# Attention probabilities turned in 32 × 32 blocks on VectorE and placed by sixteen DMAs, with the value product one unit later

## The chip, the cores and the metric

The kernel runs on one core of a Trainium2 chip. The metric is the device time of one execution, in microseconds (us). An engine's name is followed here by what it does in this kernel: TensorE (PE) multiplies and transposes, VectorE (DVE) and ScalarE (ACT) move results out of PSUM and do the softmax, GpSimd (POOL) does small sums, splits and gathers, and SyncE (SP) issues transfers.

## The reference, cut to what matters

Three small layers with adapters produce x (8 sequences of 128 rows, 512 columns); an attention with a paged cache follows. The part around the change is, for each of 8 sequences and each of 8 key heads (4 query heads share one key head):

```python
k_all = concatenate([kc, k], axis=1)          # 512 cached keys and 128 new ones
v_all = concatenate([vc, v], axis=1)
scores = einsum('bqhd,bkhd->bhqk', q, k_all) * SCALE
scores = where(valid, scores, -1e30)
probs = softmax(scores, axis=-1)
attn = einsum('bhqk,bkhd->bqhd', probs, v_all)
out = attn.reshape(bsz, seqlen, -1) @ Wo.T    # summed over the heads
```

with q and k projected from x, normalized by their root mean square and rotated. The result is added to x.

## The kernel before

The attention runs over 64 units, a unit being one sequence and one key head with its 4 query heads. Each engine has its own instruction stream, a loop over the units whose body is that engine's `step`; the order in each is written out by hand, and semaphores tie them together. A float32 product that needs full precision is made of three float32r products (`three`): each operand is split in a rounded high part and the rest (`..._hi`, `..._lo`). ScalarE writes the high part of a PSUM tile and VectorE the rest.

In step n TensorE computes the scores of two heads (`score_pair`, 12 products), eight of the twelve products of the next unit's queries, the scores of the other two heads, the other four query products, the output product of unit n−1 (`put_out`, 12 products), and the transposes of unit n's probabilities (`turn_probs`, five chunks of keys by four heads, 20 in all) alternating with the value products (`values`, 15 of 512 columns). Between these it projects the next unit's new key and value (`project_new_key`, 12 products of 256 columns) and transposes its rotated queries and key (`turn_rotated`) and the cached keys of the unit after (`turn_cached`). The turned probabilities pass through two PSUM banks, `ps_ring`; ScalarE copies each (`chunk_high`, tile pt_hi) and VectorE subtracts (`chunk_low`, tile pt_lo). The softmax takes, for each head, a masked minimum on VectorE (`lowest`, L1112), the exponential on ScalarE (`exps`, L622), the reciprocal of the sum on VectorE (`inverse`), and the scaling on ScalarE (`normalize`, L627). The keys' path is key square on ScalarE (L585), `variances` and `rotate_key` on VectorE (L1061 to L1073), a power on GpSimd (`norm_factors`), `scale_key` on ScalarE (L603), the transpose, then `rotated_high` on ScalarE and `rotated_low` on VectorE. SP loads the next unit's x_s (L335) when its key product is done, and a chunk of later weights (L338). Line 1028 is VectorE's subtraction of any tile (`rest`), L582 ScalarE's copy of any tile.

Of the kernel before, what the change touches and what calls it, by code (L numbers as in the profile page):

```python
# [13 lines left out]
P = 128  # L14
# [17 lines left out]
AHEAD = B + 1  # L32
THETA = 10000.0
# [13 lines left out]
def build(nc, x, x_t, ids0, ids1, ids2, table, lens, w0_t, bias0, lora_a, lora_b, w1_t, w2_b, w2_a,  # L47
          w_qkvo, q_norm, k_norm, k_rows, v_rows, inv_freq, row_in_table, ident_in, out):
    ctx = ExitStack()
    with ctx:  # L50
# [142 lines left out]
        with ExitStack() as p2:  # L193

            rot_a = sb("rot_a", [P, GROUP + 1, D], scope=p2)
# [13 lines left out]
            v_hi = sb("v_hi", [P, CH, D], F32R, scope=p2)  # L209
            v_lo = sb("v_lo", [P, CH, D], F32R, scope=p2)  # L210
            prob = sb("prob", [P, GROUP, KEYS], scope=p2)
            pt_hi = sb("pt_hi", [P, CH, GROUP * P], F32R, scope=p2)
            pt_lo = sb("pt_lo", [P, CH, GROUP * P], F32R, scope=p2)
            ot_hi = sb("ot_hi", [P, GROUP * P], F32R, scope=p2)
            ot_lo = sb("ot_lo", [P, GROUP * P], F32R, scope=p2)
            mask = sb("mask", [P, KEYS], scope=p2)
# [21 lines left out]
            v_hi_out, v_split, vn_hi_out, vn_lo_out = (psem(s) for s in ("v_round", "v_split", "vn_hi_out", "vn_lo_out"))  # L238
            scores, low_done, exp_done, inv_done, prob_done = (psem(s) for s in ("scores", "low_done", "exp_done", "inv_done", "prob_done"))
            p_turned, pt_hi_out, pt_lo_out = psem("p_turned"), psem("pt_hi_out"), psem("pt_lo_out")  # L240
# [9 lines left out]
            def keys_of(kt, u, lo, hi):  # L250

                return kt[:, bass.ds((u & 1) * KEYS + lo, hi - lo)]

# [3 lines left out]
            with nc.Block() as block:  # L257
                @block.sync
                def _(sp):
# [71 lines left out]
                    def step(n, weights, last, finished):  # L331
                        if not last:
                            sp.wait_ge(kv_proj, n + 1)
                            sp.nop(nofuse=True)
                            sp.dma_start(x_s[:, :, :].bitcast(F32), xt_dram[bass.ds((n + 1) & 7, 1), :, :, :].rearrange("a p s c -> p (a s) c")).then_inc(x_s_in, 16)  # L335
                        if weights:
                            sp.wait_ge(w_split, n + AHEAD)
                            sp.dma_start(w_raw[:, 0, :], w_qkvo[bass.ds(n + AHEAD, 1), :, :].rearrange("a p c -> p (a c)")).then_inc(w_raw_in, 16)  # L338
                        if finished:
                            sp.wait_ge(y_added, n)  # L340
                            sp.nop(nofuse=True)
                            sp.dma_start(out[bass.ds((n - 1) & 7, 1), :, :].rearrange("a p c -> p (a c)"),
                                         y[:, bass.ds((n - 1) & 7, 1), :].rearrange("p a c -> p (a c)")).then_inc(out_in, 16)

                    sp.wait_ge(xt_stored, 32)
                    step(0, True, False, False)
                    sp.wait_ge(xt_stored, 16 * B)
                    with sp.Fori(1, UNITS - AHEAD) as n:
                        step(n, True, False, False)
                    with sp.Fori(UNITS - AHEAD, UNITS - B + 1) as n:  # L350
                        step(n, False, False, False)
                    with sp.Fori(UNITS - B + 1, UNITS - 1) as n:
                        step(n, False, False, True)
                    step(UNITS - 1, False, True, True)
                    step(UNITS, False, True, True)
# [3 lines left out]
                def _(pool):  # L359
# [108 lines left out]
                    def step(n, weights, keys, last):  # L468

                        vl = v_lo[:, 0:CCH, :].rearrange("p c d -> p (c d)")  # L470
                        vh = v_hi[:, 0:CCH, :].rearrange("p c d -> p (c d)")
# [3 lines left out]
                        pool.wait_ge(v_hi_out, n + 1)  # L475
                        nc.gpsimd.tensor_tensor(vl, v_raw[:, :], vh.bitcast(F32), ALU.subtract).then_inc(v_split, 1)  # L476
                        if not last:
                            next_values(n + 1)
                        if keys:
                            next_keys(n + 2)  # L480
# [7 lines left out]
                    with pool.Fori(0, UNITS - AHEAD) as n:  # L488
# [4 lines left out]
                    step(UNITS - 1, False, False, True)  # L493

                @block.scalar
                def _(act):
# [108 lines left out]
                    def cached_high(u, first=False):  # L605
# [3 lines left out]
                        copy(keys_of(kt_hi, u, 0, CACHE), ps_ring[:, 0, :]).then_inc(kc_hi_out, 1)  # L609
# [6 lines left out]
                    def out_high(u):  # L616
                        act.wait_ge(pv_done, u + 1)
                        copy(ot_hi[:, :], ps_o[:, :]).then_inc(ot_hi_out, 1)
# [10 lines left out]
                    def chunk_high(n, c, bank):  # L629
                        act.wait_ge(p_turned, CH * n + c + 1)  # L630
                        copy(pt_hi[:, c, :], ps_ring[:, bank, :]).then_inc(pt_hi_out, 1)

                    def step(n, keys, last, first=False):
                        if first:
                            cached_high(1, first=True)
                        else:
                            out_high(n - 1)
# [627 lines left out]
```

## Time and profile before

| | |
|---|---|
| median of 3 runs | 1242.81 us (1242.17 to 1243.01) |
| the profiled execution | 1239.95 us |
| its span, first to last instruction | 1238.1 us |
| busy: TensorE, VectorE, ScalarE, GpSimd | 98%, 74%, 69%, 44% |
| mean granted clock of TensorE | 0.993 of full speed |
| data moved by DMA | 109.5 MB, 88 GB/s on the mean |

The span is what the profile shows of one execution; the time of that execution is a little longer, and the runs that give the median were other executions. Busy means that an instruction of the engine was in progress; matmuls overlap, so a busy TensorE says that it was never without one. Each row of the timeline gives the start, the length, the engine and the line, and the output and inputs.

### The profile page before, as it was taken

The page shows a single profiled execution, that of the slowest core. Times are in us where ns is not written, and L with a number is a line of the kernel's source. Part 1 is how long each engine was busy: PE and PEld are TensorE (multiplying, and loading weights), DVE is VectorE, ACT ScalarE, POOL GpSimd, SP SyncE. Part 2 cuts the span into 40 slices and gives each one's busy share as a digit, 9 for nine tenths or more (in the row PEclk, how much of TensorE's full clock was granted, in tenths as well). Part 3 has the DMA queues.
Part 4 walks back from the last instruction along what each step waited for, and adds up shares of the span by engine and source line. Part 5 has one row for each costly group of instructions (what it writes and reads, how often), then busy time and mean ns, then how long its engine had stood idle before and what let it go on. Part 6 is the DMA issues. An engine that isn't in the chain of part 4 may idle for free.

```text
span 1238.1 us, 28992 instructions
## 1 busy us (share of the span) xinstructions
PE 1212.0 (98%) x7072; PEld 1038.2 (84%) x7072; DVE 918.8 (74%) x2295; ACT 853.2 (69%) x2170; POOL 545.5 (44%) x570
## 2 busy tenths in 40 slices
PE   7998999999999999999999999999999999999997
PEld 4565888888888888888888888888888888888885
DVE  2336778777778777787787877877778777777774
ACT  2233777777777777777777777777777777767774
POOL 7761444445444444444444444444544445333430
PEclk9998999999999999999999999999999999999999
DMA  6673222222222222222122222222222222112210
GB/s 193 232 255 107 78 67 78 89 89 67 75 80 89 89 62 80 80 89 89 61 74 87 89 86 65 72 89 89 78 67 77 89 89 69 63 59 85 85 52 25
DMA packets 37607, 109.50 MB, mean 88 GB/s; under 512 B 7512, under 2 KB 7640, under 8 KB 36570
## 3 DMA queue, kind: packets, MB, share of 16 engines
q1 hardware_dynamic: 25288, 68.44, 16.1%
q0 software_dynamic: 11152, 36.72, 10.4%
q10 hardware_dynamic: 1154, 4.19, 0.9%
q8 instruction: 6, 0.10, 0.0%
q14 instruction: 7, 0.06, 0.0%
HBM read 103.03 MB, written 6.29 MB: 88 GB/s over the span
## 4 chain that ended last, share of the span: by engine, by line
PE 96%; DVE 1%; ACT 1%; DMA 1%; issue 1%; POOL 0%; SPq 0%; DVEq 0%; ACTq 0%; POOLq 0%
PE ps_q L794 14%; PE ps_ring L858 12%; PE ps_o L694 11%; PE ps_o L696 11%; PE ps_o L695 11%; PE ps_kv L794 7%; PE ps_s L696 6%; PE ps_s L694 6%; PE ps_s L695 6%; PE ps_l L726 2%; PE ps_ring L820 2%; PE ps_q L828 2%; PE ps_t L688 1%; PE ps_l L742 1%; PE ps_h L712 1%
## 5 line engine op out<-in xcount | busy, mean ns | idle before, releaser
L622 ACT ACTIVATE prob<-prob,low 128x640 f32<-128x640 f32 x256 | 210.8, 824 | 129.0 <-DVE low L1112 128.9
L1028 DVE TENSOR_TENSOR pt_lo<-ps_ring,pt_hi 128x512 fp32r<-128x512 f32 x320 | 209.1, 686 | 87.8 <-ACT pt_hi L582 87.5
L1112 DVE CUSTOM_DVE_ANT_0 prob<-ps_s,mask,q_gain 128x640 f32<-128x640 f32 x256 | 216.3, 882 | 36.8 <-PE ps_s L696 35.0
L103 POOL TENSOR_TENSOR w_lo<-w_raw,w_hi 128x640 f32 (+1 forms) x64 | 100.2, 1565 | 263.6 <-DVE w_hi L97 262.3
L582 ACT ACTIVATE pt_hi<-ps_ring 128x512 fp32r<-128x512 f32 x320 | 181.5, 593 | 33.1 <-PE ps_ring L858 33.0
L627 ACT ACTIVATE prob<-prob,inv 128x640 f32<-128x640 f32 x256 | 196.9, 818 | 0.0
L858 PE MATMUL ps_ring<-ident,prob 128*128 128x128 f32 x1280 | 186.3, 276 | 5.1 <-DVE pt_lo L1028 2.7
L858 PEld LDWEIGHTS ps_ring<-ident,prob 128*128 128x128 f32 x1280 | 149.0, 141 | 40.3 <-DVE pt_lo L1028 9.9
L794 PE MATMUL ps_q<-w_hi,x_s 128*128 (+1 forms) x512 | 171.8, 396 | 0.0
L694 PE MATMUL ps_s<-kt_hi,qt_hi 128*128 (+1 forms) x512 | 159.4, 311 | 1.5 <-DVE low L1112 1.5
L696 PE MATMUL ps_s<-kt_hi,qt_lo 128*128 (+1 forms) x512 | 159.5, 311 | 0.0
L695 PE MATMUL ps_s<-kt_lo,qt_hi 128*128 (+1 forms) x512 | 159.1, 311 | 0.0
L476 POOL TENSOR_TENSOR v_lo<-v_raw,v_hi 128x512 fp32r<-128x512 f32 x64 | 83.4, 1302 | 154.6 <-DVE v_hi L1085 154.6
L694 PE MATMUL ps_o<-pt_hi,v_hi 128*128 128x512 f32 x320 | 147.6, 461 | 0.0
L696 PE MATMUL ps_o<-pt_hi,v_lo 128*128 128x512 f32 x320 | 126.9, 397 | 0.0
L695 PE MATMUL ps_o<-pt_lo,v_hi 128*128 128x512 f32 x320 | 125.6, 392 | 0.0
L466 POOL TENSOR_TENSOR rstd<-var,neg_half 128x5 f32<-128x5 f32 x64 | 77.4, 1209 | 85.9 <-DVE var L1061 85.8
L794 PEld LDWEIGHTS ps_q<-w_hi,x_s 128*128 128x128 f32 x512 | 95.6, 188 | 15.0
L794 PE MATMUL ps_kv<-w_hi,x_s 128*128 (+1 forms) x512 | 106.8, 293 | 0.0
L694 PEld LDWEIGHTS ps_s<-kt_hi,qt_hi 128*128 128x128 f32 x512 | 97.0, 189 | 7.5 <-DVE low L1112 1.8
L694 PE MATMUL ps_o<-w_hi,ot_hi 128*128 (+1 forms) x256 | 101.0, 394 | 1.4 <-DVE ot_lo L1028 1.4
L695 PEld LDWEIGHTS ps_s<-kt_lo,qt_hi 128*128 128x128 f32 x512 | 96.9, 189 | 5.7
(141 smaller groups left out, 2587.8 us busy)
## 6 DMA issues: line engine op xcount, KB each, us to landing
x_s<-xt_split SPq DMA_DIRECT2D x64, 512.0 KB, 3.3
w_raw<-w_qkvo_dram SPq DMA_DIRECT2D x55, 320.0 KB, 3.5
w<-w_t_dram SPq DMA_DIRECT2D x8, 1024.0 KB, 6.8
xt_split<-x3t ACTq DMA_DIRECT2D x8, 512.0 KB, 4.3
w_raw<-w_qkvo_dram POOLq DMA_DIRECT2D x9, 320.0 KB, 4.9
xbt<-x_t_dram SPq DMA_DIRECT2D x8, 256.0 KB, 2.9
xb<-x_dram SPq DMA_DIRECT2D x8, 256.0 KB, 3.7
out_dram<-y SPq DMA_DIRECT2D x8, 256.0 KB, 2.2
```

What stands on the lines that cost most here:

```text
L103: return nc.gpsimd.tensor_tensor(lo, raw, hi.bitcast(F32), ALU.subtract)
L476: nc.gpsimd.tensor_tensor(vl, v_raw[:, :], vh.bitcast(F32), ALU.subtract).then_inc(v_split, 1)
L582: return nc.scalar.activation(dst, src, ACT.Copy)
L622: nc.scalar.activation(prob[:, h, :], prob[:, h, :], ACT.Exp, bias=low[:, h:h + 1], scale=-1.0, accum_out=total[:, h:h + 1]).then_inc(exp_ ...
L627: nc.scalar.activation(prob[:, h, :], prob[:, h, :], ACT.Copy, scale=inv[:, h:h + 1]).then_inc(prob_done, 1)
L694: nc.tensor.matmul(dst, lh, rh, start=first, stop=False)
L695: nc.tensor.matmul(dst, lh, rl, start=False, stop=False)
L696: return nc.tensor.matmul(dst, ll, rh, start=False, stop=final)
L794: mm = nc.tensor.matmul(dst, x_s[:, int(i % 3 == 2), k * P:(k + 1) * P], w_rest if i % 3 == 1 else w, start=i == 0, stop=i == 3 * KT - 1)
L858: mm = nc.tensor.transpose(ps_ring[:, bank, h * P:(h + 1) * P], prob[:, h, c * P:(c + 1) * P], ident[:, :])
L1028: return nc.vector.tensor_tensor(dst, src, high.bitcast(F32), ALU.subtract)
L1112: nc.vector.tensor_tensor_reduce(out=prob[:, h, :], in0=ps_s[:, score_slot(h):score_slot(h) + KEYS], in1=mask[:, :], scale=q_gain[:, h:h + ...
```

## The change

The probabilities are no longer transposed by TensorE. VectorE turns each head's 128 × 640 probabilities in 32 × 32 blocks (`turn_blocks`), which leaves every block in the group of 32 partitions where it was, and sixteen DMAs on SP's queue (`place_blocks`: 4 source groups by 4 destination groups, each 32 partitions of 2560 bytes) carry the blocks to where a transpose would have put them, in one of two halves of `prob_t` (alternating by unit). The source `blocks` is a single buffer, so the first turn of the next unit waits for all sixteen.

The value product takes `prob_t` and the values as plain float32, with one product in place of three, in two halves of two heads (256 columns) and five chunks each: ten instructions. It belongs to the unit before and stands last in TensorE's step; the output product belongs to two units before. Its second half uses the PSUM bank `ps_o1`, in which the cached keys of the next unit are turned before, so it waits until VectorE has taken those (`kc_lo_out`). The splits of the values (v_hi, v_lo, on VectorE and GpSimd) and of the turned probabilities are gone; ScalarE copies the new value to `v_next` and GpSimd from there to `v_new`. The gather of a unit's cached values moves from the step before to the step in which they are used. The query products are no longer cut in eight and four but all stand between the score pairs; the key product and the turning of the cached keys follow the second score pair. On ScalarE the squares move ahead of the exponentials of heads 2 and 3. On SP the x_s load is asked for before the sixteen transfers of the same step.

The diff, cut to its core. Blank lines and, outside TensorE's step, most removed lines are left out; the functions that they stand in are printed above. Indentation is shortened.

```diff
-ps_ring = pb("ps_ring", [P, 2, 512], p2)
+ps_x = pb("ps_x", [P, 512], p2)
+ps_o0 = pb("ps_o0", [P, 512], p2)
 ps_q = pb("ps_q", [P, 512], p2)
 ps_kv = pb("ps_kv", [P, 512], p2)
-ps_o = pb("ps_o", [P, 512], p2)
+ps_o1 = pb("ps_o1", [P, 512], p2)
+ps_o = (ps_o0, ps_o1)
...
+PAIR = 2 * P
+RUN = CH * GROUP * BLOCK
+def place_block(issuer, n, a, j):
+    issuer.dma_start(prob_t[j * BLOCK:(j + 1) * BLOCK, bass.ds((n & 1) * NB * RUN + a * RUN, RUN)],
+             blocks[a * BLOCK:(a + 1) * BLOCK, j, :, :, :].rearrange("p c h q -> p (c h q)")).then_inc(pt_in[j], 16)
+def turned_probs(u, c, pair):
+    half = prob_t[:, bass.ds((u & 1) * NB * RUN, NB * RUN)]
+    return half.rearrange("p (a c h q) -> p h a c q", a=NB, c=CH, h=GROUP)[:, 2 * pair:2 * pair + 2, :, c, :]
+def next_value(u):
+    return v_next[:, bass.ds((u & 1) * D, D)]
...
+def place_blocks(n, first=False):
+    sp.wait_ge(blocks_turned, GROUP * (n + 1))
+    sp.nop(nofuse=True)
+    if not first:
+        sp.wait_ge(pv_done, 2 * (n - 1))
+        sp.nop(nofuse=True)
+    for a in range(NB):
+        for j in range(NB):
+            place_block(sp, n, a, j)
...
+def step(n, inputs, weights, finished, first=False):
+    if inputs:
+        next_input(n + 2)
     if weights:
+        next_weights(n + 1)
+    place_blocks(n, first)
     if finished:
+        store_out(n - 2)
...
-    pool.wait_ge(v_split, u)
+    pool.wait_ge(pv_done, 2 * u)
...
+def move_new_value(u, values):
+    pool.wait_ge(vn_out, u + 1)
+    if values:
+        pool.wait_ge(pv_done, 2 * u)
+    pool.nop(nofuse=True)
+    nc.gpsimd.tensor_copy(v_new[:, :], next_value(u)).then_inc(vn_moved, 1)
+def step(n, weights, keys, last, first=False, second=False):
+    if not first:
+        move_new_value(n - 1, not second)
+        if not second:
+            next_values(n - 1)
     if weights:
         pool.wait_ge(w_rounded, n + AHEAD + 1)
         weight_low(n + AHEAD, w_raw[:, 0, :]).then_inc(w_split, 1)
     if not last:
         sum_queries(n + 1)
         norm_factors(n + 1)
+    if keys:
+        next_keys(n + 2)
...
+def step(n, last, head=True, out=True, first=False):
+    if head:
+        out_high(n - 2, 1, first=first)
     exps(n, 0)
     exps(n, 1)
     normalize(n, 0)
     normalize(n, 1)
+    if not last:
+        query_squares(n + 1, range(GROUP))
+        key_squares(n + 1)
+        new_value(n + 1, first=not out)
     exps(n, 2)
     exps(n, 3)
     normalize(n, 2)
+    if not last:
+        scale_key(n + 1)
+        cached_high(n + 1, ps_o1, first=not out)
     normalize(n, 3)
     if not last:
         rotated_high(n + 1)
+    if out:
+        out_high(n - 1, 0, first=not head)
...
+def values(u, cached, first=False):
+    pe.wait_ge(v_in, 16 * (u + 1))
+    pe.wait_ge(vn_moved, u + 1)
+    for j in range(NB):
+        pe.wait_ge(pt_in[j], 16 * NB * (u + 1))
+    if not first:
+        pe.wait_ge(ot_lo_out, 2 * u)
+    for pair in (0, 1):
+        if pair == 1:
+            pe.wait_ge(kc_lo_out, cached)
+        for c in range(CH):
+            v = v_raw[:, c * D:(c + 1) * D] if c < CCH else v_new[:, :]
+            mm = nc.tensor.matmul(ps_o[pair][:, 0:PAIR], v, turned_probs(u, c, pair),
+                                  start=c == 0, stop=c == CH - 1)
+        mm.then_inc(pv_done, 1)
...
+def step(n, last, out=True, pv=True, first=False):
     pe.wait_ge(qt_lo_out, n + 1)
     pe.wait_ge(kc_lo_out, n + 1)
     score_pair(n, 0)
     if not last:
         project_queries(n + 1)
     score_pair(n, 1)
     if not last:
-        project_queries_rest(n + 1)
-    if not first:
-        put_out(n - 1)
-    early, late = range(GROUP - 1), (GROUP - 1,)
-    pe.wait_ge(prob_done, GROUP * n + GROUP - 1)
-    turn_probs(n, 0, 1, early)
-    pe.wait_ge(kc_lo_out, n + 1 if last else n + 2)
-    turn_probs(n, 1, 0, early)
-    pe.wait_ge(prob_done, GROUP * n + GROUP)
-    turn_probs(n, 0, 1, late)
-    turn_probs(n, 1, 0, late)
-    if not last:
         project_new_key(n + 1)
-    pe.wait_ge(v_split, n + 1)
-    pe.wait_ge(vn_lo_out, n + 1)
-    if not first:
-        pe.wait_ge(y_added, n)
-    pe.wait_ge(pt_lo_out, CH * n + 1)
-    turn_probs(n, 2, 1)
-    values(n, 0)
-    pe.wait_ge(pt_lo_out, CH * n + 2)
-    turn_probs(n, 3, 0)
-    values(n, 1)
-    pe.wait_ge(pt_lo_out, CH * n + 3)
-    turn_probs(n, 4, 1)
+        turn_cached(n + 1, ps_o1, 2 * (n - 1) if out else None)
+    if out:
+        put_out(n - 2, first=first)
     if not last:
         turn_rotated(n + 1)
-    values(n, 2)
-    if keys:
-        pe.wait_ge(pt_lo_out, CH * n + 4)
-        turn_cached(n + 2)
-    values(n, 3)
-    values(n, 4)
+    if pv:
+        values(n - 1, n + 1 if last else n + 2, first=not out)
...
+def turn_blocks(n, h, first=False):
+    dve.wait_ge(prob_done, GROUP * n + h + 1)
+    if h == 0 and not first:
+        for j in range(NB):
+            dve.wait_ge(pt_in[j], 16 * NB * n)
+    nc.vector.transpose(blocks[:, :, :, h, :].rearrange("p j c q -> p c j q"),
+                        prob[:, h, :].rearrange("p (c j k) -> p c j k", c=CH, j=NB)).then_inc(blocks_turned, 1)
+def step(n, weights, last, head=True, out=True, first=False):
+    if head:
+        out_low(n - 2, 1)
+    dve.wait_ge(mask_set, n + 1)
+    dve.wait_ge(gain_done, n + 1)
+    if not first:
+        dve.wait_ge(blocks_turned, GROUP * n)
+    lowest(n, 0)
+    lowest(n, 1)
     if weights:
         weights_high(n)
     inverse(n, 0)
     inverse(n, 1)
+    if not last:
+        rotate_queries(n + 1)
+        rotate_queries_rest(n + 1)
     lowest(n, 2)
     lowest(n, 3)
+    turn_blocks(n, 0, first)
     if not last:
         variances(n + 1)
         rotate_key(n + 1)
+    turn_blocks(n, 1)
+    inverse(n, 2)
+    inverse(n, 3)
+    if head:
+        add_out(n - 2)
+    turn_blocks(n, 2)
     if not last:
         rotated_low(n + 1)
         gains(n + 1)
+    turn_blocks(n, 3)
+    if not last:
+        cached_low(n + 1, ps_o1)
+    if out:
+        out_low(n - 1, 0)
```

## Rows read from the trace of the kernel before

**Rows 1.** The page: busy us (share) of each engine; the chain that ended last.

```profile
PE 1212.0 (98%) x7072; PEld 1038.2 (84%) x7072; DVE 918.8 (74%) x2295; ACT 853.2 (69%) x2170; POOL 545.5 (44%) x570
...
PE 96%; DVE 1%; ACT 1%; DMA 1%; issue 1%; POOL 0%; SPq 0%; DVEq 0%; ACTq 0%; POOLq 0%
```

**Rows 2.** TensorE's timeline, one unit: start us, us, engine, line, operation.

```profile
606.76 0.28 PE L694 MATMUL ps_s<-kt_hi,qt_hi 128*128 x1
...
613.11 0.40 PE L694 MATMUL ps_o<-w_hi,ot_hi 128*128 x1
...
615.87 1.03 PE L858 MATMUL ps_ring<-ident,prob 128*128 128x128 f32 x8
616.66 0.36 PE L794 MATMUL ps_kv<-w_hi,x_s 128*128 x1
...
618.04 0.28 PE L794 MATMUL ps_kv<-w_hi,x_s 128*128 x1
```

**Rows 3.** VectorE's timeline, the same unit.

```profile
612.76 0.88 DVE L1112 CUSTOM_DVE_ANT_0 prob<-ps_s,mask,q_gain 128x640 f32<-128x640 f32 x1
...
618.76 0.17 DVE L1061 TENSOR_SCALAR var<-sq 128x5 f32<-128x5 f32 x1
...
619.69 0.68 DVE L1028 TENSOR_TENSOR pt_lo<-ps_ring,pt_hi 128x512 fp32r<-128x512 f32 x1
...
622.51 0.69 DVE L1028 TENSOR_TENSOR qt_lo<-ps_q,qt_hi 128x512 fp32r<-128x512 f32 x1
623.12 0.28 DVE L1028 TENSOR_TENSOR kt_lo<-ps_kv,kt_hi 128x128 f32 x1
623.32 0.16 DVE L1078 TENSOR_SCALAR q_gain<-rstd 128x4 f32<-128x4 f32 x1
623.39 0.48 DVE L1032 TENSOR_SCALAR mask<-pos,len_f 128x512 f32<-128x512 f32 x1
623.95 0.49 DVE L97 CAST w_hi<-w_raw 128x640 f32 x1
```

**Rows 4.** ScalarE's timeline, the same unit.

```profile
611.04 1.54 ACT L627 ACTIVATE prob<-prob,inv 128x640 f32<-128x640 f32 x2
...
618.36 0.28 ACT L585 ACTIVATE junk<-ps_kv 128x128 f32<-128x128 f32 x1
...
620.31 0.40 ACT L603 ACTIVATE rot<-key_sum,rstd 128x128 f32<-128x128 f32 x1 [0.80 <-POOL rstd L466]
620.62 1.15 ACT L582 ACTIVATE pt_hi<-ps_ring 128x512 fp32r<-128x512 f32 x2
621.72 0.60 ACT L582 ACTIVATE qt_hi<-ps_q 128x512 fp32r<-128x512 f32 x1
```

**Rows 5.** Timelines: the first score product of units 0 and 63; ScalarE's last normalizations.

```profile
119.49 0.56 PE L694 MATMUL ps_s<-kt_hi,qt_hi 128*128 128x256 f32 x1
...
1212.42 0.28 PE L694 MATMUL ps_s<-kt_hi,qt_hi 128*128 128x256 f32 x1
...
1220.08 1.53 ACT L627 ACTIVATE prob<-prob,inv 128x640 f32<-128x640 f32 x2
```

**Rows 6.** TensorE's timeline in the layers before the attention.

```profile
43.23 3.70 PE L726 MATMUL ps_l<-w,x1t 128*128 128x512 f32 x8
46.86 1.12 PE L742 MATMUL ps_l<-a,h 16*128 16x512 f32 x2
```

**Rows 7.** SP's timeline: four issues in a row at the start.

```profile
1.28 1.84 SPq L298 DMA_DIRECT2D y<-w_t_dram  x4
```

**Rows 8.** DMA issues: count, KB each, us from issue to landing.

```profile
x_s<-xt_split SPq DMA_DIRECT2D x64, 512.0 KB, 3.3
...
a<-lora_a_dram SPq DMA_DIRECT2D x8, 32.0 KB, 2.4
```

**Rows 9.** TensorE's timeline; then a stretch, PEclk its granted clock.

```profile
130.51 1.24 PE L858 MATMUL ps_ring<-ident,prob 128*128 128x128 f32 x8 [2.10 <-ACT prob L627]
...
130.00:135.00 5.00, 4.49 (x25) 4.41 (x26) 2.29 (x8) 3.56 (x14) 1.58 (x2) 0.66 0.21 60
```

More of the change, by code:

```diff
@@ L345, in _ @@
                     sp.wait_ge(xt_stored, 32)
-                    step(0, True, False, False)
+                    next_input(1)
+                    next_weights(0)
                     sp.wait_ge(xt_stored, 16 * B)
-                    with sp.Fori(1, UNITS - AHEAD) as n:
-                        step(n, True, False, False)
[L350 to L353, printed above, removed]
@@ L487, in _ @@
                     next_keys(1)
-                    with pool.Fori(0, UNITS - AHEAD) as n:
+                    step(0, True, True, False, first=True)
+                    step(1, True, True, False, second=True)
+                    with pool.Fori(2, UNITS - AHEAD) as n:
                         step(n, True, True, False)
@@ L627, in normalize @@
                         nc.scalar.activation(prob[:, h, :], prob[:, h, :], ACT.Copy, scale=inv[:, h:h + 1]).then_inc(prob_done, 1)
[L629 to L637, printed above, removed]
+                    def step(n, last, head=True, out=True, first=False):
+                        if head:
+                            out_high(n - 2, 1, first=first)
                         exps(n, 0)
                         exps(n, 1)
-                        act.wait_ge(kv_proj, n + 1)
-                        copy(v_hi[:, CCH, :], ps_kv[:, D:2 * D]).then_inc(vn_hi_out, 1)
                         normalize(n, 0)
                         normalize(n, 1)
+                        if not last:
+                            query_squares(n + 1, range(GROUP))
+                            key_squares(n + 1)
+                            new_value(n + 1, first=not out)
                         exps(n, 2)
@@ L854, in put_out @@
                         mm.then_inc(out_proj, 1)
-                    def turn_probs(n, c, bank, heads=range(GROUP)):
-                        for h in heads:
-                            mm = nc.tensor.transpose(ps_ring[:, bank, h * P:(h + 1) * P], prob[:, h, c * P:(c + 1) * P], ident[:, :])
-                        if h == GROUP - 1:
-                            mm.then_inc(p_turned, 1)
-                    def values(n, c):
-                        pe.wait_ge(pt_lo_out, CH * n + c + 1)
-                        mm = three(ps_o[:, :], (v_hi[:, c, :], v_lo[:, c, :]), (pt_hi[:, c, :], pt_lo[:, c, :]),
-                                   c == 0, c == CH - 1)
-                        if c == CH - 1:
-                            mm.then_inc(pv_done, 1)
@@ L870, in step @@
-                    def step(n, keys, last, first=False):
-                        if first:
-                            pe.wait_ge(kc_lo_out, 1)
-                            turn_cached(1)
+                    def step(n, last, out=True, pv=True, first=False):
                         pe.wait_ge(qt_lo_out, n + 1)
@@ L1188, in _ @@
                     set_mask(0)
-                    step(0, True, False, first=True)
-                    with dve.Fori(1, UNITS - AHEAD) as n:
+                    step(0, True, False, head=False, out=False, first=True)
+                    step(1, True, False, head=False)
+                    with dve.Fori(2, UNITS - AHEAD) as n:
                         step(n, True, False)
```

203 lines of the change are left out of this document (92 added, 111 removed).

## The prediction

> **What bounds the kernel now.** I read the page's busy shares and its chain of waits first [rows 1]: TensorE is busy 98% of the span and is 96% of the chain that ended last, while VectorE and ScalarE are busy 74% and 69%. Next came one unit on TensorE's timeline [rows 2]: its products follow one another without a gap. The reader is to see the stretches: from the first score product to the first output product (both score pairs and all twelve query products) 613.11 − 606.76 = 6.35 us; the twelve output products 2.76 us (0.23 us each); eight transposes of probabilities 0.79 us (0.10 each); the twelve key/value products from 616.66 to the end of the last, 618.04 + 0.28 = 618.32, 1.66 us. Then VectorE's and ScalarE's timelines of the same unit [rows 3, 4], for the length of each step and the time from the start of an instruction to the start of the one that waited for it. The first score product of unit 0 starts at 119.49 and that of unit 63 at 1212.42 [rows 5]: 17.35 us a unit over 63 steps. Because TensorE never waits, a unit costs the sum of its products. The question about the change is whether that stays so.
>
> **What the change takes from TensorE.** Per unit go 20 transposes at 0.10 to 0.11 us (2.1 us) and 15 float32r value products at 0.23 (3.45) [rows 2], 5.6 us in all. In come ten plain float32 products of 256 columns. The layers before the attention show this kind with 512 columns: four of them (eight records) start at 43.23 and the next group at 46.86, 0.91 us each [rows 6]. Half the columns is 0.45 us, ten are 4.5 us. TensorE's own work falls by 1.1 us, to 16.2 us a unit. That would be a time of 119.5 + 63 × 16.2 + 31.5 + 4.8, about 1176 us, if nothing else bound (the last terms are derived below).
>
> **What it does to the order.** TensorE now ends a step with the second half of the previous unit's value product. It shares its bank with the turned cached keys, so it waits for cached_low(n+1), which VectorE runs after the fourth turn_blocks(n). The next unit's scores are queued behind that half on TensorE. So everything from the scores of unit n to VectorE's last steps stands in one line. I add it up from the first score product of step n (time 0):
> - scores, queries (all twelve, now between the two score pairs), scores, then the key/value product: 6.35 + 1.66 + 0.04 for the hand-over = 8.05 [rows 2, 4].
> - ScalarE: the key square now stands ahead of exps 2 and 3, with the copy of the new value behind it: 0.28 + 0.29 = 8.62 [rows 4] (a 128-column copy takes about what the square takes).
> - VectorE: variances and rotate_key, 619.69 − 618.76 = 0.93 [rows 3], to 9.55; then turn_blocks 1. No row shows a block turn. It reads and writes 640 columns in SBUF. Bounds: the cast of 640 columns takes 0.49, the masked-minimum over 640 columns 0.88 [rows 3]. A two-operand step of 512 columns occupies the engine 0.61 (0.81 with the 128-column one of about 0.20 behind it), which scaled to 640 is 0.76. I take 0.76, since such a turn should pass one column after another. At 10.3 inverse 2 can start.
> - ScalarE: 0.17 later normalize 2 (0.73 of the pair's 1.54), scale_key 0.31, cached_high 0.50, normalize 3 0.73, rotated_high until VectorE can start 0.79 [rows 3, 4]: 13.5. The exponentials 2 and 3 (at 8.5 and 9.3, 0.83 each) fit beside turn_blocks 1. The output product, from about 8.3 to 11.1, and its add lie beside this too.
> - VectorE: rotated_low 0.81, gains 0.07, turn_blocks 3 0.76, cached_low 0.69 and an allowance of 0.15 until TensorE's product starts: 16.0 [rows 3].
> - TensorE: five products of 0.45, 2.25: 18.3.
>
> A unit thus costs 18.3 us, 2.1 more than TensorE's work and 0.95 more than now. With turns of 0.49 (two on the line, and less for what they hide) it would be 17.7, with 0.88 18.5; both are above 17.35. Most of the five evictions that leave ScalarE (pt_hi, about 0.55 each [rows 4]) and VectorE (0.6 each) buy nothing on this line: the four turns take their place on VectorE, and ScalarE waits about a microsecond for the key product. The vector copy v_hi, GpSimd's subtraction v_lo and the small v_lo go at no gain, since none ends a wait on the line; GpSimd's new copy and its gather of values at the start of the step have until 12 us, its pieces with the landing of 3.3 us being over by about 5.
>
> **The sixteen transfers.** Each moves 32 partitions × 2560 B = 82 KB, 1.31 MB a unit. They are issued on SP after turn_blocks 3; the first turn of the next unit waits for all of them, because it overwrites their source. Four issues in a row start 0.46 us apart [rows 7]; small transfers land in 2.4 us and the 512 KB one in 3.3 [rows 8]. So they take 16 × 0.45 + 0.1 + 2.5 = 9.8 us. Turn 3 ends at about 15.2. Turn 0 of the next unit is due when the fourth masked minimum ends, 18.3 + 7.8 = 26.1 (it starts at 612.76, 6.0 after the first score product [rows 2, 3], here one us later for the four query products moved ahead, and takes 0.8): 10.9 us of room, 1.1 to spare. Above that each microsecond goes into the unit whole. The loads of x_s (next_input) and weights are queued behind them on SP; the issues end 4 us into the next step, the key product that next_input also waits for at 8, so they lose nothing. Upper bound from rows: 2.4 to 3.3 us for 480 KB more is 0.15 us for 82 KB over 128 partitions; if 32 partitions are served four times slower, 0.6 us, 16 of them with landing are 12.2 us. I take the issue rate and keep 12.2 for the range. The Trainium skill (SBUF — State Buffer, Door 1: The DMA port swizzle) says that 32 partitions reach half of the 16 ports, measured at 189 GB/s. An estimate by it is 0.43 us for each transfer, as long as its issue, so that the x_s, weight and gather traffic on the same engines would decide; no run here shows such a transfer yet. That sentence speaks against the change.
>
> **Sum.** 119.5 to the first scores (unchanged) + 63 × 18.3 = 1152.9. From the last unit's first score product to the end is 1238.1 − 1212.4 = 25.7 now. Then: probabilities normalized as now at 1221.6 (+9.2 [rows 5]), last turn +0.8, transfers 9.8, ten products 4.5, eviction in two parts 0.9, output 2.9 + 0.3, add 0.7, store 2.4: 31.5. Span 1303.9. The profiled execution took 1239.95, 1.85 over its span, and the median of the runs lies 2.9 above it: 1308.7, so 1309 us. Unit 0 pays its cold start as now. The break-even is 17.25 us a unit.
>
> **Rivals.**
> - *The line is as added up*: 1309, with the bounds of the turns 1271 to 1322. Chance 0.58.
> - *The transfers bind.* For it: 1.1 us of room only, 1.3 MB of other traffic a unit by the tiles' sizes, the gather of values within these 10 us. Against: issue 0.45 each. At 12.2 the unit costs 12.2 + 7.4 = 19.6 (turn 0's 0.76 and from there the line above to the end of turn 3, 15.2 − 8.6), time 1394 with the later end; at 11.5, 1347. Served slower still by the other traffic, 1420. Chance 0.22.
> - *Block turns at half rate*, 1.5 us. Now three of them are on the line: 20.4 a unit, 1441. No row shows one. The Trainium skill (VectorE: DVE Perf Modes, The three transpose paths) gives 311 ns for 128 columns; an estimate by it for 640 is 1.56 us. Against, every VectorE row here passes about a column a nanosecond. Chance 0.07.
> - *Faster: plain float32 products of 256 columns pass at the float32r rate*, about 0.13 us (twelve key/value products of 256 columns in 1.66 [rows 2]). Pair 1 then costs 0.65 instead of 2.25, the unit 16.7, time 1208. It decides from 0.24 us a product down. Against: 0.91 at 512 columns [rows 6]. With whatever else makes the line at least 1.05 us shorter than I read it, chance 0.09; a further 0.01 for no change.
> - *The clock falls.* TensorE would idle 2.1 us a unit in two or three gaps. After 128.4 to 130.5, 2.1 us without work, the mean granted clock was 0.66, partly at the lower level of 1.2 GHz [rows 9]. One such stretch a unit makes about 3.4 us of products take twice as long, half of it on the line: 20.0 a unit, 1416. The gaps are split, so 0.03.
>
> Chances: slower 0.88, within 0.2% 0.03, faster 0.09 (0.2% is about what a measurement of this kernel can tell; a spread of the first case or of the fast one near the break-even gives the 0.03). The range 1268 to 1420 holds the first case with its bounds, the second and the clock's. It leaves out the fast case, no change and the slow turns, 0.17, and some edges of the rest. The likeliest case alone spans 1271 to 1322.
>
> **What would show it.** In the profile after: TensorE near 88% busy, with idle time before the second value half put down to VectorE's kt_lo, and a little before the rotated transposes; the chain passing through VectorE and ScalarE; ScalarE's key square waiting about 1 us for ps_kv; block turns near 0.76 to 0.85 us; plain products 0.45 us apart; SP issues 0.45 us apart; no VectorE wait on the transfers. If turn 0 waits for a transfer, the second case holds and my landing time is wrong. If TensorE stays gapless at 16.2 us a unit, I have read the order wrongly.

## The result and the profile after

The changed kernel takes 1412.07 us (median of 4 runs, 1410.91 to 1414.47), against 1242.49 for the kernel before, run in between. The ratio is 1.1374, with a 95% interval of 1.1348 to 1.14: 170 us slower. The recorded forecast was 1309, 67 us slower, in a range of 1268 to 1420.

The page of the changed kernel, busy shares and chain, to be laid beside [rows 1]:

```profile
PE 1219.1 (86%) x6112; PEld 1013.1 (72%) x6112; DVE 855.5 (61%) x2167; ACT 685.0 (49%) x1914; POOL 475.6 (34%) x570
SPq 39%; issue 19%; DVE 11%; PE 11%; DMA 9%; ACT 7%; DVEq 2%; ACTq 0%; POOL 0%; POOLq 0%
L1156 DVE STREAM_TRANSPOSE blocks<-prob 128x640 f32<-128x640 f32 x256 | 215.1, 841 | 109.2 <-DMA prob_t<-blocks 92.5
```

TensorE has lost its 96% of the chain; SP's queue, which before had 0% of it, holds 39%, and the block turns wait 92.5 us for transfers. SP's timeline shows two units:

```profile
676.20 10.49 SPq L264 DMA_DIRECT2D prob_t<-blocks  x16
...
695.91 10.50 SPq L264 DMA_DIRECT2D prob_t<-blocks  x16
...
715.62 10.49 SPq L264 DMA_DIRECT2D prob_t<-blocks  x16
```

The batches start 715.62 − 695.91 = 19.71 us apart, and 695.91 − 676.20 = 19.71 before that: that is a unit. Between 400 and 1000 us most units take just this and some up to 20.1. Sixteen issues take 10.5 us. VectorE's timeline between those batches, the four turns and the two subtractions about the last:

```profile
705.53 0.88 DVE L1137 CUSTOM_DVE_ANT_0 prob<-ps_s,mask,q_gain 128x640 f32<-128x640 f32 x1
...
707.99 0.84 DVE L1156 STREAM_TRANSPOSE blocks<-prob 128x640 f32<-128x640 f32 x1 [1.57 <-DMA prob_t<-blocks]
708.76 0.13 DVE L1092 TENSOR_SCALAR var<-sq 128x5 f32<-128x5 f32 x1
...
709.58 0.84 DVE L1156 STREAM_TRANSPOSE blocks<-prob 128x640 f32<-128x640 f32 x1
...
711.36 0.85 DVE L1156 STREAM_TRANSPOSE blocks<-prob 128x640 f32<-128x640 f32 x1 [0.25 <-ACT prob L692]
713.50 0.69 DVE L1058 TENSOR_TENSOR qt_lo<-ps_q,qt_hi 128x512 fp32r<-128x512 f32 x1 [1.29 <-ACT kt_hi L640]
...
714.38 0.84 DVE L1156 STREAM_TRANSPOSE blocks<-prob 128x640 f32<-128x640 f32 x1
715.14 0.65 DVE L1058 TENSOR_TENSOR kt_lo<-ps_o,kt_hi 128x512 f32 x1
```

A loop can be read off. Turn 0 starts at 707.99, turn 3 is done at 715.14 (taken here, as in the prediction, as the start of the next step), the first issue follows at 715.62: 7.63 us. From the first issue to the turn 0 that waits for the last transfer it is 707.99 − 695.91 = 12.08. Together 19.71, the whole unit. The chain, in order of time, shows the last pieces of the 12.08, the second column being the length:

```profile
704.55 0.53 SPq L264
705.21 0.53 SPq L264
705.88 1.99 DMA prob_t<-blocks
```

Issues follow each other every 0.66 us (an instruction of 0.53 and the register instructions between), and the last lands 1.99 us after its start: 15 × 0.664 + 1.99 + 0.12 = 12.07.

TensorE's timeline holds a second surprise. It shows the two halves of the value product, first in the unit before, then in this one:

```profile
692.05 0.63 PE L881 MATMUL ps_q<-ident,rot 128*128 128x128 f32 x4 [2.15 <-ACT rot L661]
...
692.79 1.99 PE L914 MATMUL ps_o<-prob_t,v_raw 128*128 x8
...
696.22 1.99 PE L914 MATMUL ps_o<-prob_t,v_raw 128*128 x8 [1.01 <-DVE kt_lo L1058]
...
711.76 0.63 PE L881 MATMUL ps_q<-ident,rot 128*128 128x128 f32 x4 [2.12 <-ACT rot L661]
712.23 0.37 PE L882 MATMUL ps_kv<-ident,rot 128*128 128x128 f32 x1
712.53 3.53 PE L914 MATMUL ps_o<-prob_t,v_raw 128*128 x8
715.90 0.59 PE L914 MATMUL ps_o<-prob_t,v_new 128*128 x2
716.33 1.89 PE L914 MATMUL ps_o<-prob_t,v_raw 128*128 x8
```

and the windows over the latter two (window, length, busy time of the five engines, granted clock, DMA share, GB/s):

```profile
713.00:715.00 2.00, 2.00 (x6) 1.54 (x6) 1.50 (x4) 0.47 (x2) 0.00 (x0) 0.50 0.31 111
717.00:719.00 2.00, 2.00 (x13) 1.82 (x12) 0.77 (x2) 0.31 (x1) 0.05 (x1) 1.00 0.52 123
```

In this unit TensorE idles 2.12 us, and then runs at 0.50, the lower level of 1.2 GHz: four products (eight records) take 3.53 us in the first half, and 1.89 in the second, which is at full clock. This does not come in every unit. In the unit before, the gap is 2.15 us, the clock stays at 1.00, and the first half takes 1.99 us. Of the 30 units between 400 and 1000 us, 18 have a slow first half (2.95 to 3.67 us) and 12 a fast one (1.99), and the mean granted clock there is 0.95. So two suspects stood: the issues on SP and the clock. The profile already speaks for the first: the unit with the fast half is 19.71 us from batch to batch like the one with the slow half. With the clock full, the second half stands and waits 1.01 us for kt_lo instead.

### The profile page after: what moved, and what is told of

Read it like the earlier page. It is cut to its first block, busy times and chain, and to the rows that moved or that the text cites. A ratio compares the mean times of both kernels' runs of the same rounds, so it can differ in the third digit from the quotient of the medians.

```text
span 1411.1 us, 29468 instructions
## 1 busy us (share of the span) xinstructions
PE 1219.1 (86%) x6112; PEld 1013.1 (72%) x6112; DVE 855.5 (61%) x2167; ACT 685.0 (49%) x1914; POOL 475.6 (34%) x570
## 4 chain that ended last, share of the span: by engine, by line
SPq 39%; issue 19%; DVE 11%; PE 11%; DMA 9%; ACT 7%; DVEq 2%; ACTq 0%; POOL 0%; POOLq 0%
SPq L264 38%; DMA prob_t<-blocks 9%; DVE blocks L1156 5%; ACT kt_hi L640 3%; PE ps_l L782 2%; ACT prob L692 2%; ACT rot L661 2%; DVE kt_lo L1058 1%; DVE rot_b L1101 1%; PE ps_o L914 1%; PE ps_q L881 1%; DVE rot_a L1099 1%; PE ps_q L850 1%; PE ps_t L744 1%; DVEq L1058 1%
## 5 line engine op out<-in xcount | busy, mean ns | idle before, releaser
L914 PE MATMUL ps_o<-prob_t,v_raw 128*128 (+1 forms) x1024 | 304.4, 450 | 33.4 <-DVE kt_lo L1058 24.6
L914 PEld LDWEIGHTS ps_o<-prob_t,v_raw 128*128 128x128 f32 x1024 | 223.9, 228 | 95.2 <-issue 57.4
L1156 DVE STREAM_TRANSPOSE blocks<-prob 128x640 f32<-128x640 f32 x256 | 215.1, 841 | 109.2 <-DMA prob_t<-blocks 92.5
L750 PE MATMUL ps_s<-kt_hi,qt_hi 128*128 (+2 forms) x512 | 172.0, 336 | 6.2 <-issue 3.4
L752 PE MATMUL ps_s<-kt_hi,qt_lo 128*128 (+2 forms) x512 | 160.2, 313 | 0.0
L751 PE MATMUL ps_s<-kt_lo,qt_hi 128*128 (+2 forms) x512 | 160.0, 312 | 0.0
L1058 DVE TENSOR_TENSOR ot_lo<-ps_o,ot_hi 128x256 fp32r<-128x256 f32 x128 | 53.9, 421 | 162.3 <-ACT ot_hi L640 162.3
L511 POOL TENSOR_TENSOR rot<-rot_a,rot_b 128x512 f32<-128x512 f32 x64 | 83.5, 1304 | 89.0 <-DVE rot_b L1084 89.0
L750 PE MATMUL ps_x<-w_hi,ot_hi 128*128 (+1 forms) x256 | 106.1, 414 | 2.0 <-DVE ot_lo L1058 2.0
L750 PEld LDWEIGHTS ps_s<-kt_hi,qt_hi 128*128 128x128 f32 x512 | 97.4, 190 | 11.7 <-issue 3.6
L850 PE MATMUL ps_q<-w_lo,x_s 128*128 (+1 forms) x256 | 101.2, 395 | 0.0
```

The costliest lines, as they stand in the source:

```text
L750: nc.tensor.matmul(dst, lh, rh, start=first, stop=False)
L751: nc.tensor.matmul(dst, lh, rl, start=False, stop=False)
L752: return nc.tensor.matmul(dst, ll, rh, start=False, stop=final)
L850: mm = nc.tensor.matmul(dst, x_s[:, int(i % 3 == 2), k * P:(k + 1) * P], w_rest if i % 3 == 1 else w, start=i == 0, stop=i == 3 * KT - 1)
L914: mm = nc.tensor.matmul(ps_o[pair][:, 0:PAIR], v, turned_probs(u, c, pair), start=c == 0, stop=c == CH - 1)
L1156: nc.vector.transpose(blocks[:, :, :, h, :].rearrange("p j c q -> p c j q"), prob[:, h, :].rearrange("p (c j k) -> p c j k", c=CH, j=NB)). ...
```

## The experiments

All ratios are to the kernel before, run on the same chip in the same series (medians 1243.69 to 1244.89). The first theory in all of them: the single source `blocks` ties turn 0 to the issues of the unit before, and beneath that lies the recorded line of 18.3 us a unit. The rivals: the data of the transfers, the clock, or another wait. The changed kernel (1412.07) was measured in a series of its own, so where a run is set against it in microseconds, 1 to 2 us are the difference of the series.

**e1_double: a second source buffer.** Turns wait for the placing of the unit before last.

```diff
-dve.wait_ge(pt_in[j], 16 * NB * n)
+dve.wait_ge(pt_in[j], 16 * NB * (n - 1))
+half = blocks[:, odd * NB * RUN:(odd + 1) * NB * RUN]      # odd = n & 1
 ...
+sp.wait_ge(pt_in[j], 16 * NB * n)                           # before placing unit n
```

The cut leaves out that VectorE's loop is unrolled by two, and that two scratch tiles (`key_sum`, `junk`) lie in other tiles to make room for the second buffer.

> Two buffers for the turned blocks, so the first turn of a unit waits for the transfers of two units before instead of one; the sixteen transfers and their issue stay. My account (the transfers of 12.8 us bind, behind them the line of 18.3 us): the unit falls from 19.9 to 18.2 to 18.6 us, the time to 1305 to 1335 us, turn 0 waits for no transfer, SP still issues one per 0.66 us. Rival (something else costs the 1.6 us that the turn waits, or the traffic slows everything): stays within 1% of 1412. Rival (the clock is the loss): the stretch with the low clock behind the 2.1 us gap stays only if the gap stays; by my account the gap shrinks to about 0.5 us and the granted clock rises from 0.94 to 0.99.

Measured: 1306.35 us, ratio 1.0497 (1.0466 to 1.0528). Its SP timeline and waits (of 400 to 1000 us; total, times, longest):

```profile
612.96 11.06 SPq L264 DMA_DIRECT2D prob_t<-blocks  x16
...
631.08 1.30 SPq L264 DMA_DIRECT2D prob_t<-blocks  x2
```

```profile
PE ps_o L918 <- DVE kt_lo L1062: 32.6, 33, 1.0
```

The unit is 631.08 − 612.96 = 18.12 us though the sixteen issues take longer here (0.69 each). No wait of VectorE on a transfer is left; TensorE waits 1.0 us a unit for kt_lo, the last step of the recorded line. The mean granted clock rises from 0.94 to 0.99. With the transfers hidden in this way the recorded 1309 nearly comes out.

**e2_static: fixed destination addresses, one buffer.** SP's loop is unrolled by two so that the home is a constant.

```diff
-prob_t[j * BLOCK:(j + 1) * BLOCK, bass.ds((n & 1) * NB * RUN + a * RUN, RUN)]
+prob_t[j * BLOCK:(j + 1) * BLOCK, odd * NB * RUN + a * RUN:odd * NB * RUN + (a + 1) * RUN]
```

> The same sixteen transfers with destination addresses fixed at build time (SP's loop unrolled by two units), one buffer for the blocks as in the changed kernel. If an issue takes 0.66 us because of its register address, it falls to about 0.45, the transfers to 9.5 us, and the time to 1310 to 1345. If 0.66 us is what a transfer between two groups of 32 partitions costs SP in itself, the spacing stays above 0.55 us and the time above 1370.

Measured: 1369.46 us, 1.1002 (1.0958 to 1.1046). Its SP timeline:

```profile
602.14 10.04 SPq L264 DMA_DIRECT2D prob_t<-blocks  x16
...
621.18 10.04 SPq L264 DMA_DIRECT2D prob_t<-blocks  x16
```

```profile
613.76 0.85 DVE L1159 STREAM_TRANSPOSE blocks<-prob 128x640 f32<-128x640 f32 x1 [0.94 <-DMA prob_t<-blocks]
```

The issues now follow each other every 0.63 us with no register work between: the hoped-for 0.45 did not come, so the register work is not what makes them long. The instruction itself has become longer, 0.59 for 0.53 at the median; why, no run shows. The time is half a microsecond under the 1370 that the second theory had as its floor. The unit is 19.04, and the same loop gives it: turn 0 started at 613.76, so 11.62 from the first issue and 7.42 from there to the next. 0.67 less a unit is 42 us of the 43 gained.

**e3_double_static: both at once** (one run).

> Both together. If the transfers no longer bind with two buffers, this adds nothing: within 0.5% of the kernel with two buffers alone, and its SP timeline shows the spacing of fixed addresses on both sides.

Measured: 1305.39 us. With the transfers covered, shorter issues buy nothing.

**e4_keys_early: the last link of the line moved.** e3, with `cached_low` ahead of the third turn.

```diff
+if not last: cached_low(n + 1, ps_o1)
 turn_blocks(n, odd, 2)
 ...
 turn_blocks(n, odd, 3)
-if not last: cached_low(n + 1, ps_o1)
```

> Both together, and cached_low (VectorE's part of the turned cached keys) moved from behind turn 3 to ahead of turn 2. If the line through cached_low to the second half of the value product is what binds without the transfers, taking two turns (1.5 us) out of it shortens the unit by about 1.4 us, to 16.8 us, and the time to 1205 to 1235, below the kernel before. If TensorE's own work or the rotated path binds, it stays at the two-buffer kernel's time within 1%.

Measured: 1226.59 us, 0.9872 (0.9845 to 0.9899), 1.3% below the kernel before. The wait for kt_lo is gone; TensorE has one left, for the scaled key:

```profile
621.13 0.48 PE L757 MATMUL ps_x<-w_hi,ot_hi 128*128 x1
...
624.71 0.63 PE L888 MATMUL ps_q<-ident,rot 128*128 128x128 f32 x4 [0.58 <-ACT rot L668]
...
625.48 1.99 PE L921 MATMUL ps_o<-prob_t,v_raw 128*128 x8
```

**e5_half_bytes: bytes or issues?**

```diff
-blocks[...].rearrange("p c h q -> p (c h q)")
+blocks[...].rearrange("p c h q -> p (c h q)")[:, 0:RUN // 2]     # both ends; from unit 2 on
```

> The changed kernel, with each of the sixteen transfers cut to its first 320 of 640 columns from unit 1 on (41 KB instead of 82 KB); the other half of the turned probabilities of unit 0 stays in its home, so later units compute with stale values there: the work left out is half of the placing. First theory, a transfer's place in SP's queue costs what its issue costs, whatever it carries: the issues stay 0.63 to 0.66 us apart, only the landing shortens by a few tenths, the time is 1385 to 1412 us. Rival, the data set the pace (32 partitions of 2560 B pass slowly, and the queue is held up by them): the spacing falls towards 0.46, the wait of VectorE's first turn goes away, and the time is 1305 to 1350.

The code sends units 0 and 1 whole, so the halves are left out from unit 2 on, and not from unit 1.

Measured: 1397.17 us, 1.1237 (1.1211 to 1.1264). Its timeline of SP, the wait of turn 0, and the window 400 to 1000 us:

```profile
608.87 10.49 SPq L264 DMA_DIRECT2D prob_t<-blocks  x16
```

```profile
620.75 0.84 DVE L1156 STREAM_TRANSPOSE blocks<-prob 128x640 f32<-128x640 f32 x1 [1.06 <-DMA prob_t<-blocks]
```

```profile
400.00:1000.00 600.00, 526.30 (x2728) 448.99 (x2728) 390.48 (x1015) 315.89 (x896) 205.61 (x245) 0.96 0.34 104
```

The DMA engines' share falls from 0.49 to 0.34, and the sixteen issues take 10.49 us as before, to the hundredth. Only the last landing is 0.2 shorter (11.88 for the way, 620.75 − 608.87, and a unit of 19.52). The data were not the limit.

**e6_split_queues: four of the sixteen on ScalarE's queue.**

```diff
 for a in range(NB - 1):                      # SP: 12
     for j in range(NB): place_block(sp, n, a, j)
 ...
 out_high(n - 1, 0, first=not head)           # ScalarE
+act.wait_ge(blocks_turned, GROUP * (n + 1))
+act.wait_ge(pv_done, 2 * (n - 1))
+for j in range(NB): place_block(act, n, NB - 1, j)
```

> The changed kernel with the last four of the sixteen transfers issued by ScalarE, after its first output eviction of the step, and twelve left on SP. First theory, each queue's issues cost 0.66 us of that queue and nothing of the other's: SP's last issue comes 2.6 us earlier, the way from the end of turn 3 to turn 0 falls from 12.8 to about 10.2 us, under the 10.9 of room, VectorE's wait on the transfers (1.4 to 1.6 us a unit) goes away and the unit falls to 18.3 us: 1300 to 1335 us. Rival, the transfers themselves share one limit: the time stays within 1395 to 1415. ScalarE's own four issues, some 2.4 us, stand ahead of its second output eviction and could cost up to 0.5 us a unit (1340).

Measured: 1304.55 us, 1.0496 (1.0458 to 1.0534). SP's and ScalarE's timelines:

```profile
608.91 7.98 SPq L264 DMA_DIRECT2D prob_t<-blocks  x12
```

```profile
608.78 2.50 ACTq L264 DMA_DIRECT2D prob_t<-blocks  x4
```

All bytes move, at 0.51 of the DMA engines' time, and 108 us go by using two queues, with one source buffer as before. The wait is gone, the unit is 18.12, and ScalarE's 2.5 us cost nothing here. With e5 this settles it: what binds is how fast one queue takes such transfers, and not the bytes that they carry.

**e7_early_keys_only: e4's move on the changed kernel itself.**

> The changed kernel with one source buffer as it is, and cached_low moved ahead of turn_blocks 2 on VectorE. With two source buffers the same move gave 79 us. Here the transfers bind: the first turn of a unit waits for them, and the move only puts 0.69 us more between turn 0 and turn 3. Theory: no gain, 19.9 to 20.6 us a unit, 1410 to 1455 us. Rival, the line of scores and keys binds here too: it gains as much as there, 1330 to 1345 us.

Measured: 1419.46 us, 1.1416 (1.1388 to 1.1444), its SP timeline:

```profile
616.88 10.49 SPq L264 DMA_DIRECT2D prob_t<-blocks  x16
...
636.74 8.50 SPq L264 DMA_DIRECT2D prob_t<-blocks  x13
```

What gave 79 us in e4 gives nothing here; that it costs anything is not shown, since the interval overlaps that of the changed kernel (1.1348 to 1.14). The loop runs from turn 0 through turn 3 and the transfers, and the keys are not in it. In this unit it grew by only 0.15 us, to 19.86, not by the 0.69 of the subtraction: VectorE stood idle 1.29 us before qt_lo in any case, and most of the moved step fills that hole.

**e8_filled_gap: the clock held up.** Sixteen transposes of the identity on TensorE ahead of `turn_rotated`.

```diff
+for _ in range(16):
+    nc.tensor.transpose(ps_o0[:, 3 * D:4 * D], ident[:, :], ident[:, :])
 turn_rotated(n + 1)
```

> The changed kernel, with sixteen transposes of the identity (128 columns each, about 0.11 us, 1.7 us together, into a free bank) put on TensorE ahead of turn_rotated, where it idles 2.1 us a unit. They add work that nobody uses. They fit into the gap, so by themselves they cost nothing. The granted clock should then stay at 1.0 and pair 0 of the value product take 1.9 instead of 3.5 us. First theory, little of the slow clock lies on the line (rotated transposes 0.63 instead of 0.36 us, and what follows on ScalarE and VectorE; pair 0 itself ends before the keys are ready): 0.2 to 0.4 us a unit, 1387 to 1400 us. Rival, it is on the line whole: 1.0 us or more a unit, 1330 to 1350. If the time stays within 2 us of 1412, the clock costs nothing here.

Measured: 1406.18 us, 1.1303 (1.1274 to 1.1332). Its TensorE timeline:

```profile
708.59 1.91 PE L942 MATMUL ps_o<-ident 128*128 128x128 f32 x16
710.89 0.63 PE L881 MATMUL ps_q<-ident,rot 128*128 128x128 f32 x4 [0.40 <-issue]
...
711.63 1.99 PE L914 MATMUL ps_o<-prob_t,v_raw 128*128 x8
...
715.06 1.99 PE L914 MATMUL ps_o<-prob_t,v_raw 128*128 x8 [1.01 <-DVE kt_lo L1060]
```

The granted clock over 400 to 1000 us is 1.00 (0.95 in the changed kernel), and pair 0 takes 1.99. Yet the batches on SP still start 19.71 apart, and only some 6 us are gained in all (9 by the ratios), less than the 12 that my first theory asked for at least. In the two traces the way from the batch of unit 1 to that of unit 62 is 1203.5 us here and 1208.2 in the changed kernel, 0.08 a unit: here every unit between 400 and 1000 us takes 19.71, and the units of up to 20.1 are gone. The slow products were covered nearly whole: at full clock pair 1 stands and waits 1.01 us for kt_lo, as in the fast units of the changed kernel, and that is the time which the slow pair 0 had used.

**e9_all_partitions: where an issue's length comes from.**

```diff
-issuer.dma_start(prob_t[j * BLOCK:(j + 1) * BLOCK, bass.ds((n & 1) * NB * RUN + a * RUN, RUN)],
-                 blocks[a * BLOCK:(a + 1) * BLOCK, j, :, :, :].rearrange("p c h q -> p (c h q)"))
+part = (NB * a + j) * (RUN // NB)
+issuer.dma_start(prob_t[:, bass.ds((n & 1) * NB * RUN + part, RUN // NB)],
+                 flat[:, part:part + RUN // NB])
```

> The changed kernel, with the same sixteen transfers of 82 KB from blocks to prob_t, but each over 128 partitions and 160 columns, straight across: what is left out is that a block lands in its own partitions. It tells what the 0.53 us of an issue come from, since an issue costs them with half the bytes too. First theory, they come from the small number of partitions with long rows: the issues fall to 0.35 us as for x_s, 0.47 apart, the transfers' way from turn 3 to turn 0 is 9.8 us or less, and the time is 1300 to 1335 us, as the recorded prediction had it. Rival, they come from source and destination both lying in SBUF, or from the descriptors that 16 columns of a block need: 0.53 us stay, and the time is 1400 to 1415 us.

Measured: 1378.8 us, 1.1076 (1.1046 to 1.1105). Its SP timeline:

```profile
605.99 10.16 SPq L266 DMA_DIRECT2D prob_t<-blocks  x16
616.83 0.35 SPq L358 DMA_DIRECT2D x_s<-xt_split  x1
```

Neither the 1300 to 1335 of the theory nor the 1400 to 1415 of the rival was hit. The issue falls from 0.53 only to 0.49 to 0.52 with 128 partitions, while the x_s load in the next line, six times the bytes from DRAM, takes 0.35. The landing is shorter as well, and 11.62 for the whole way gives the unit of 19.26. The few partitions are a small part of it. That both ends lie in SBUF is left as a possible reason, but nothing here varied it alone, and the transfers differ from the x_s load in their shape too.

**e10_scale_key_first: e4 without its last wait.**

```diff
+if not last: scale_key(n + 1)
 normalize(n, 2)
-if not last: scale_key(n + 1)
 cached_high(n + 1, ps_o1)
```

> The kernel of e4 (two source buffers, fixed addresses, cached_low ahead of turn_blocks 2), with scale_key ahead of normalize 2 on ScalarE. In e4 TensorE's only wait left is 0.56 us a unit for the scaled key. Theory: TensorE is the bound again at 16.2 to 16.4 us a unit, 1190 to 1210 us. Rival: normalize 2, now 0.3 us later, delays turn 2 and turn 3 and takes the gain back: 1220 to 1235 us.

Measured: 1164.48 us, 0.9375 (0.9348 to 0.9402), beyond the theory's 1190. TensorE's timeline, in which no row has a wait any more:

```profile
600.92 0.47 PE L758 MATMUL ps_s<-kt_hi,qt_hi 128*128 x1
...
609.23 0.48 PE L758 MATMUL ps_x<-w_hi,ot_hi 128*128 x1
...
612.09 0.60 PE L889 MATMUL ps_q<-ident,rot 128*128 128x128 f32 x4
...
612.63 1.91 PE L922 MATMUL ps_o<-prob_t,v_raw 128*128 x8
...
614.81 1.89 PE L922 MATMUL ps_o<-prob_t,v_raw 128*128 x8
...
616.78 0.47 PE L758 MATMUL ps_s<-kt_hi,qt_hi 128*128 x1
```

The unit is 616.78 − 600.92 = 15.86 us. I had gone by the idle time that the view gave in e4, 0.58. From start to start the gap was larger: first output product to first rotated transpose 624.71 − 621.13 = 3.58 there and 2.86 here, and rotated to pair 0 0.77 there and 0.54 here. That is 0.95 a unit, and (1226.59 − 1164.48) / 63 = 0.99 went. Ends of matmuls are modelled, and an idle time reckoned from them came out short here.

**e11_split_and_early_keys: one buffer, both cheap edits** (e6 and e7 together).

> The changed kernel with its one source buffer, four of the sixteen transfers on ScalarE and cached_low ahead of turn_blocks 2. The move alone gained nothing (19.85 us a unit), since the transfers bound. With 2.6 us less of them on SP that loop should take 19.85 - 2.6 = 17.25 us a unit, and the line of the keys 16.8: 1248 to 1260 us, just about the kernel before, with VectorE's first turn still waiting some 0.4 us for transfers. Rival: the wait is gone whole and the time is that of e4, 1225 to 1235 us.

Measured: 1262.35 us, 1.0147 (1.0128 to 1.0166), a unit of 627.24 − 609.84 = 17.40 from batch to batch on SP; 2 us above the range and with another wait than I had named. Its ScalarE timeline, and VectorE's:

```profile
609.71 2.51 ACTq L264 DMA_DIRECT2D prob_t<-blocks  x4
612.63 0.39 ACT L640 ACTIVATE ot_hi<-ps_o 128x256 fp32r<-128x256 f32 x1 [3.21 <-issue]
```

```profile
613.05 0.42 DVE L1064 TENSOR_TENSOR ot_lo<-ps_o,ot_hi 128x256 fp32r<-128x256 f32 x1 [2.78 <-issue]
```

No turn waits for a transfer. Now ScalarE's own issues, harmless at 18.12 us a unit, hold back its second output eviction, and VectorE waits 2.78 us for it ahead of the next unit's masked minimum. No run took this wait away alone, so that it makes up the 0.5 us a unit over e4's 16.87 (the mean there) is argued and not shown.

## Why the prediction went as it did

The direction was right, the line was right, and one term was wrong, which made the second rival the true case.

- **The term that failed: the sixteen transfers, "16 × 0.45 + 0.1 + 2.5 = 9.8 us".** From the end of turn 3 it is 0.48 + 15 × 0.664 + 1.99 + 0.12 = 12.55. The landing was shorter than assumed (2.11 for 2.5), the first issue came later behind turn 3 (0.48 for 0.1), and the issues stood 0.664 apart for 0.45, which makes 15 × 0.664 = 9.96 to the last one for the 7.2 of 16 × 0.45: this is the part that counts. The 0.46 came from four loads at the start of the kernel [rows 7], which are other transfers. The room, "10.9 us", was right: in e1 turn 3 ends at 612.27 and the next turn 0 starts at 623.15, 10.88. So 12.55 − 10.88 = 1.67 had to show, and 1.57 does as turn 0's wait.
- **The likeliest case, 18.3 us a unit and 1309.** It is what lies beneath: 18.12 and 1306.35 in e1, 1304.55 in e6. That the time comes so near is in part luck. In e1's trace the 63 units take 8.9 us less than 63 × 18.3, while unit 0 starts 3.9 later and the end is 7.0 longer than in the sum. The key subtraction as its last link is shown by e4, which takes it away.
- **The second rival, 19.6 us and 1394.** Its loop of 12.2 + 7.4 is the measured 12.08 + 7.63. But I reached the 12.2 by supposing 32 partitions to be served slowly, and e5 rules that out: half the bytes, the same issues. The rival had the right loop and the wrong cause; that its 12.2 lies near the 12.08 is luck. The Trainium skill (SBUF — State Buffer, Door 1: The DMA port swizzle) has 32 partitions at half the ports; e9, with all of them, shortens the way by 0.46 of 12.08 us, so little of the price lies there.
- **The clock rival, "0.03", 20.0 us and 1416.** The clock does fall, in 18 of the 30 units between 400 and 1000 us, which I took for unlikely because I had split the idle time over several gaps; the late turn makes one gap of about 2.1 us of it. Its price was wrong in the other direction: half of it "on the line", I wrote; e8 gives about 0.1 us a unit. That 1412 lies near its 1416 is chance.
- **Plain products, 0.45.** At full clock a half of five takes 614.81 − 612.63 = 2.18, 0.44 each. The fast case is out.
- **TensorE's own work, 16.2.** Too much by 0.34: 15.86 in e10.
- **The sum.** From 123.78 to 1371.79 it is 63 × 19.81, and the end takes 39.3. Of the 107 us that the span has over the 1303.9 of the sum, 63 × 1.51 = 95 are the unit's, 4.3 a later start of unit 0 (I had called it unchanged), and 7.8 the end. There the last unit's first issue comes 13.3 us after its first score product for the 10.1 of the sum, in part because turn 0 waits 1.77 us for transfers once more; the products follow the first issue after 11.7 for 9.7; and they run at 0.50 of the clock for their first 4 us, after 7.25 us without work.
- **Signs.** TensorE at 86% for 88, the chain off TensorE. The sign "if turn 0 waits for a transfer, the second case holds and my landing time is wrong" was right in its first half; it was the issues. The idle time before the second value half is there in the units at full clock (1.01 at 696.22) and in e1 and e8, and hidden by the slow pair 0 in the others. ScalarE's wait for the key product was 0.40, not 1 us.

The change thus lost its gain twice. The products it saves are real (17.35 to 15.86 us a unit where TensorE waits for nothing), but the placing first closed a loop through a single buffer and one queue, worth 106 us (e1), and behind that the order of VectorE's and ScalarE's steps held TensorE for another 142 (e1 to e10).

## What to carry to other kernels

The sixteen small transfers were priced by the issue, and an issue's length must be taken from a transfer of the same kind; a row from another part of the kernel is a bound, not a value. Where the margin is 1.1 us and the term is sixteen times something, an error of 0.07 us in each uses it up, so such a case deserves more than 0.22. Follow each buffer round its loop (last write, transfer, next write) and compare that loop with the line, since moving steps of one does nothing while the other is longer: the same move gave 79 us in e4 and nothing in e7.

## What the runs showed of the hardware

- A transfer from SBUF to SBUF holds its queue's sequencer for 0.529 us, with 82 or 41 KB, and 0.49 to 0.52 over 128 partitions; ScalarE's queue takes 0.55. The 512 KB load from DRAM takes 0.35. Fixed addresses save 0.03 of the spacing of 0.66; the instruction then takes 0.59 (e2).
- Such transfers land 2.0 us after the issue begins, at half the time of the DMA engines in use.
- With a gap of 1.7 to 2.2 us in each unit the granted clock fell to 0.50 in 18 of 30 units and stayed at 1.00 in 12, so the length of the gap alone does not tell: behind one of 2.15 us it stayed, behind one of 2.12 it fell. With gaps of 1.5 us (e2, 400 to 1000 us) and of 0.4 us (e8) it stayed at 1.00 throughout.
- VectorE turns 128 × 640 float32 values in 32 × 32 blocks in 0.84 us, one following another after 0.77.
